# Identity products in TensorE's waits: one-head layers, and the scatter and gathering around layer 2's experts

## The reference

```python
# L1: gated attention over the context, one head of 128 features, 8 batches of 256 tokens
x = x + _L1_xattn_ref(_layernorm(x), ctx_1024, ctx_1024, Wgq, bgq, Wgk, bgk, w_gate, b_gate, Wh, bh)
...
# L2: causal attention over the context, one head
Q, K, V = q @ Wq, k @ Wk, v @ Wv
scores = where(causal, -inf, Q @ K.T / sqrt(128));  out = softmax(scores) @ V
# L2: 16 experts, two per token, at most 160 rows an expert
padded = zeros((16 * 160 + 1, 128)).at[slot].set(repeat(xf, 2, axis=0))   # the scatter
h = gelu(einsum('ecd,edf->ecf', padded, w1));  out_padded = einsum('ecf,efd->ecd', h, w2)
out = sum over the two choices of out_padded[slot] * weight               # the gathering
# L3: dilated attention: inside each segment softmax(x x^T / sqrt(128)) x, one head, divided by 4
x = x + _L3_attn_ref(_layernorm(x))
```

## Time and profile before

| | |
|---|---|
| time, median of 3 runs | 2066.54 us (2065.91 to 2067.85) |
| profiled execution | 2069.29 us, of which the trace's span is 2067.6 us |
| busy, share of the span | PE 80%, DVE 44%, ACT 34%, POOL 21% |
| granted TensorE clock, mean over the span | 0.901 of full speed |
| L1x begins | at 816.0 us of the span |
| L2x begins | at 1239.4 us |
| L2f begins (scatter), and its last product begins its group | at 1322.6 us; at 1453.6 us |
| L3a begins | at 1505.0 us |

### The profile page before, as it was taken

How to read it: one execution, slowest core, us unless ns; L and a number is a source line. 1 busy time by engine, 2 the same in 40 slices (tenths; PEclk the granted TensorE clock), 3 DMA queues, 4 the chain that set the end, 5 groups by cost and what they waited for, 6 DMA issues and landing times. The chain is left out here.

```text
span 2067.6 us, 31792 instructions
## 1 busy us (share of the span) xinstructions
PE 1643.8 (80%) x11656; PEld 963.7 (47%) x11656; DVE 911.0 (44%) x2515; ACT 711.5 (34%) x1423; POOL 436.8 (21%) x517
## 2 busy tenths in 40 slices
PE   1899899994799998869899987136156999969998
PEld 1344434443444444545644435124042555548887
DVE  3455345533355654641256535311354555324444
ACT  1244424442176775524213444011041333422221
POOL 2534043400121110000053400320515434100000
PEclk8999999997999998969999998567576999969999
DMA  8200000000000000000040000011200000000000
GB/s 235 67 2 1 1 1 1 1 1 0 0 1 1 1 1 1 1 0 1 4 148 2 1 1 1 20 53 52 59 12 6 12 12 6 1 0 0 0 0 20
DMA packets 45933, 37.63 MB, mean 18 GB/s; under 512 B 3972, under 2 KB 40040, under 8 KB 45800
## 3 DMA queue, kind: packets, MB, share of 16 engines
q1 hardware_dynamic: 43752, 31.65, 5.1%
q0 software_dynamic: 2048, 4.20, 0.7%
HBM read 23.26 MB, written 12.58 MB: 17 GB/s over the span
## 5 line engine op out<-in xcount | busy, mean ns | idle before, releaser
L1309 ACT ACTIVATE scores_L_experts_L<-L3x_psL 128x512 f32<-128x512 f32 x128 | 76.4, 597 | 173.8 <-PE L3x_psL L1172 170.2
L1346 DVE CUSTOM_DVE_ANT_0 L3x_junk<-L3x_psS,L3x_mask_rows 128x256 f32<-128x256 f32 x224 | 86.4, 422 | 92.6 <-PE L3x_psS L1134 84.5
L1172 PE MATMUL L3x_psL<-identb,L3x_mask_parts 128*128 128x256 bf16 x768 | 96.2, 276 | 0.0
L2433 ACT ACTIVATE L3f_activated<-L3f_psG 128x512 f32<-128x512 f32 x72 | 43.0, 597 | 153.0 <-PE L3f_psU L2412 153.0
L2466 DVE TENSOR_TENSOR L3f_hidden<-L3f_activated,L3f_psU 128x512 f32<-128x512 f32 x72 | 49.6, 688 | 103.0 <-ACT L3f_activated L2433 103.0
L852 ACT ACTIVATE L0x_probs<-L0x_psL 128x512 f32<-128x512 f32 x96 | 52.1, 595 | 114.1 <-PE L0x_psL L665 78.9
L852 ACT ACTIVATE L2a_probs<-L2a_psL 128x512 f32<-128x512 f32 x96 | 52.1, 595 | 104.2 <-PE L2a_psL L663 69.4
L852 ACT ACTIVATE L0a_probs<-L0a_psL 128x512 f32<-128x512 f32 x96 | 52.1, 595 | 100.8 <-PE L0a_psL L663 65.0
L1154 PE MATMUL L3x_psL<-L3x_qm,ctx_T 32*128 32x512 f32 x256 | 73.7, 651 | 12.1 <-DVE L3x_mx L1346 11.6
L2398 PE MATMUL L3f_psY<-experts_L_L,L3f_hidden 128*128 128x128 f32 x576 | 76.9, 276 | 5.0 <-DVE L3f_hidden L2466 4.9
L1172 PEld LDWEIGHTS L3x_psL<-identb,L3x_mask_parts 128*128 128x128 bf16 x768 | 70.4, 98 | 21.5 <-issue 13.7
(11 more groups left out here) (768 smaller groups left out, 4025.8 us busy)
## 6 DMA issues: line engine op xcount, KB each, us to landing
packed_rows<-zeros SPq DMA_DIRECT2D x1, 4608.0 KB, 27.2
L2f_rows<-packed_rows SPq DMA_DIRECT2D x8, 320.0 KB, 3.6
unpacked_rows<-L2f_y SPq DMA_DIRECT2D x8, 320.0 KB, 2.7
experts_L_L<-in_L_ffn_w_dram SPq DMA_DIRECT2D x1, 2048.0 KB, 8.5
unpacked_rows<-zeros SPq DMA_DIRECT2D x1, 2048.0 KB, 25.1
scores_L_experts_L<-in_L_ffn_w_dram SPq DMA_DIRECT2D x1, 2048.0 KB, 7.9
L3x_mask_rows<-in_mask_Bx1xSxS_ff_dram SPq DMA_DIRECT2D x8, 256.0 KB, 2.7
experts_L_L<-n_L_ffn_expert_gate_dram SPq DMA_DIRECT2D x1, 1024.0 KB, 13.4
```

Of the source, the lines that this page charges most:

```text
L1172: last = nc.tensor.matmul(at[:, :, t * P:(t + 1) * P], parts[:, b % 2, i, t, u * P:(u + 1) * P], two, start=False, stop=i == PARTS - 1, sk ...
L1309: nc.scalar.activation(probs[:, half, a, k, :], psL[i % RING][:], ACT.Exp).then_inc(s_prob, 1)
L1346: last = nc.vector.tensor_tensor_reduce(out=junk[:, i, :], in0=psS[a][:, i * S:(i + 1) * S], in1=mrow[:, b % 2, t, :], scale=1.0, scalar=L ...
```

## The change

A helper `warm(n)` is added to `lone_head` and to `slot_experts`, which issues n products of the identity into a bank that is overwritten before it is next read (`psS[1]` in the one, `psU[0]` in the other). `lone_head` issues 14 ahead of `turn(0)`, three after it, three after `turn(1)`, and three after `project(0)` where there is one. `slot_experts` issues 170 ahead of `turn(0)`, that is during the scatter, and 170 after the last `down`, that is during the gathering. Nothing is removed and no data changes.

```diff
@@ lone_head, TensorE
+                def warm(n):
+                    for _ in range(n):
+                        nc.tensor.matmul(psS[1][:], mem.identb[:], mem.identb[:].unsqueeze(1).to_broadcast([P, 4, P]), start=True, stop=True)
+
                 def turn(b):
                     pe.wait_ge(s_h, b + 1)
...
+                warm(14)
                 turn(0)
+                warm(3)
                 turn(1)
+                warm(3)
                 if not dilated:
                     project(0)
+                    warm(3)
                 for i in range(B + 2):
                     if i < B:
                         score(i)
@@ slot_experts, TensorE
+                def warm(n):
+                    for _ in range(n):
+                        nc.tensor.matmul(psU[0][:], mem.identb[:], mem.identb[:].unsqueeze(1).to_broadcast([P, 4, P]), start=True, stop=True)
+
...
                 pe.wait_ge(w["late"], w["late_count"])
+                warm(170)
                 turn(0)
                 for c in range(PAIRS + 1):
                     if c + 1 < PAIRS:
                         turn(c + 1)
...
                     if c >= 1:
                         down(c - 1)
+                pe.wait_ge(s_hid, UNITS * PAIRS)
+                warm(170)
```

## The result

The changed kernel takes **2098.91 us** (median, 2097.68 to 2101.22) against 2066.51 of the kernel before on the same chip: a ratio of 1.0157, 95% interval 1.014 to 1.0175, so 32.4 us longer. I had predicted 2069.7, 2065 to 2073: the loss is ten times the one forecast. The profiled execution took 2099.03 us, span 2097.3, which is 29.7 more than the span of before.

A forecast was written before the change was run, and what follows sets the result against it. At layer 2's experts TensorE waits for GpSimd's transfers; slow-clock starts of one-head layers were winnable. Those starts lose 8.8 us, regain 5.6, long runs 0: 2066.54 + 3.2 = 2069.7 us, range 2065 to 2073.

The forecast's parts named there:

- The 170 in the scatter: Layer 2's experts: products take 39.2 us, end at 1361.8 before rows arrive at 1368.17, nothing late: 0.
- the first pair starts slow as before: Experts' first pair: TensorE idles 6.4 us after the fillers, so its transposes start at the low clock again: 0.
- The cover: Layer 2's experts: the 45.6 us of the scatter, the wait in which the 170 products were to fit.
- The 170 in the gathering: End of layer 2's experts: 36.6 us at high clock, ending near 1491, 14 us before L3a: 0.
- Long fillers: Scatter and gathering: clock never rises for identities alone, making them 27 and 22 us late, about 2119; chance 0.04.
- the five waits in the loop over pairs: Experts' pair loop: TensorE idles 4.98 to 5.08 us for a load, five times, then transposes slowly.
- The 14 ahead of the first transposes: Starts of L1x, L2x, L3a: transposes 3.1, 2.8 and 2.8 or 2.9 us late, 8.8 us lost in all.
- What the one-head layers cost in all: Three one-head starts: 8.8 us lost, 5.6 us given back by the faster clock, 3.2 us net cost.
- From there on the clock is high in both kernels and the stages run as before, shifted: After the three one-head starts: later work keeps its length and is only shifted, adding no further term.
- The rival of moved code: Layer 2's attention: moved code costs by itself, 2.8 us longer (207.5 to 210.3); no chance given.

The follow-up runs named there:

- e_control: Changed kernel without its own products; 170 identity products in the stage just ahead of the scatter, no transfers beside them: 2092.02 us.
- e_heads: Changed kernel keeping only the 14 and 3s of the one-head layers, both runs of 170 left out: 2072.69 us, ratio 1.0024 to the kernel before.
- e_scatter: Changed kernel keeping only the 170 products in the scatter: 2079.11 us, ratio 1.0058 to the kernel before.
- e_gaps: Kernel before plus only 20 products in each of five 5 us waits of the experts' pair loop: 2055.86 us, ratio 0.9953.
- e_fit: Changed kernel with both runs of 170 cut to 80 and the one-head layers' products left out: 2068.57 us, ratio 1.0008 to the kernel before.

## Why the prediction was wrong, step by step

**The 170 in the scatter, the step that failed.** "So the first pair starts slow as before: 0. The cover is the 45.6 us of the scatter." The cover was about right: the rows lay ready 45.7 us behind the stage's start. The term that failed is the length set against it, "39.2 us and end at 1361.8", in which the transfers beside the products cost nothing. That is right where nothing holds TensorE, 39.30 us in e_control; beside the indirect transfers the 170 took 62.9 us. Some 90 pass, and what is left when TensorE is released again stands ahead of the rows' transposes: 67 products, 17.3 us late. That the first pair would start slow fell with it: it started late and at the high clock.

**The 170 in the gathering.** "Nothing waits for psU by then [...]: 0." The same step: the 170 took 63.8 us instead of 36.6, since 60 products were left at 1520.5, and the stage's end waited for them, 14.2 us.

**The rivals.** Long fillers that cost about 27 and 22 us were there, at 0.04, but for a clock that does not rise; it rose (the mean of 0.91 from 1326 to 1346 above). The place and the sign were those of this rival, the mechanism was another, which I had not thought of: I took a column of instructions without a wait for work that can't stop. One reading of the earlier trace rows was off as well, and moved no term of the sum: the five waits in the loop over pairs are 4.96 to 5.31 us long in the trace of before, not 4.98 to 5.08.

**The 14 ahead of the first transposes.** In L1x the mechanism and the size are right: transposes 6.19 us behind the table load, 2.82 before, so 3.4 late (3.1 predicted), and project(1) 1.9 later (1.8 predicted). In L2x they took 4.7 us, not 5.7, 1.9 us late instead of 2.8, and score(1) came 1.3 us earlier where I had 0. In L3a they went at full clock all along, since the long run had ended just ahead (a row above): 0.2 late, and the first weigh 1.2 earlier instead of 1.4 later. Timelines of TensorE and ScalarE:

```profile
815.89 5.63 PE L1904 MATMUL L1x_psS<-identb 128*128 128x512 bf16 x14
821.35 0.38 PE L1911 MATMUL L1x_psT<-ident,L1x_h 128*128 128x128 f32 x2
...
826.96 0.65 PE L1920 MATMUL L1x_psQ<-L1x_hT,wT_L_gq 128*64 128x256 f32 x2
...
1244.05 4.88 PE L1904 MATMUL L2x_psS<-identb 128*128 128x512 bf16 x14 [2.43 <-PEq L88]
1248.76 0.38 PE L1911 MATMUL L2x_psT<-ident,L2x_h 128*128 128x128 f32 x2
...
1256.14 0.46 PE L1944 MATMUL L2x_psS<-L2x_kT,L2x_qT 128*128 128x128 f32 x2 [0.61 <-ACT L2x_kT L2057]
...
1539.36 0.38 PE L1911 MATMUL L3a_psT<-ident,L3a_h 128*128 128x128 f32 x2
...
1545.81 1.16 PE L1982 MATMUL L3a_psO<-L3a_h,L3a_eT 128*128 128x128 f32 x8 [0.46 <-ACT L3a_eT L2074]
```

```profile
815.16 1.28 ACT L2032 ACT_TABLE_LOAD   x1 [7.82 <-PEq L88]
...
1244.01 1.28 ACT L2032 ACT_TABLE_LOAD   x1 [4.79 <-PEq L88]
...
1536.30 1.28 ACT L2032 ACT_TABLE_LOAD   x1 [70.49 <-PEq L88]
```

With steps of 0.425 and 0.215 us, 5.46 and 4.71 us are 12 and 8 products ahead of the rise. The prediction had quoted the Trainium skill (TensorE: Matmul & The Clock Gate, Part 1) on that number's changing from run to run, and set it aside; here it changes from layer to layer.

**What the one-head layers cost in all.** By e_heads 6.2 us, interval 2.5 to 7.6, where I had 3.2: inside, but not from the places that I had summed. "From there on the clock is high in both kernels and the stages run as before, shifted" is what doesn't hold. Stage lengths in us, from one table load to the next:

| stage | before | after | e_heads | e_scatter | e_gaps | e_fit |
|---|---|---|---|---|---|---|
| L1x | 57.00 | 58.91 | 58.90 | 56.98 | 59.15 | 59.18 |
| L2a | 207.51 | 210.30 | 210.34 | 207.51 | 210.55 | 210.57 |
| L2x | 45.76 | 44.42 | 44.41 | 45.73 | 43.66 | 43.65 |

Layer 2's attention, untouched, is 2.8 us longer in the changed kernel. The rival of moved code in e_heads' expectation would have had it so, but e_gaps and e_fit, which have no product ahead of that layer, show the same, and e_scatter, which has none either, does not. In it the clock falls where it held before (windows of 1 us, before and after, the same place in the program):

```profile
1069.00:1070.00 1.00, 1.00 (x10) 0.23 (x6) 0.47 (x2) 0.00 (x0) 0.00 (x0) 1.00 0.00 0
```

```profile
1071.00:1072.00 1.00, 1.00 (x8) 0.00 (x0) 0.30 (x1) 0.00 (x0) 0.00 (x0) 0.50 0.00 0
```

Two such falls, from 1070 to 1073.4 and from 1199.7 to 1203.1, are 6.8 us at half the clock. At most 3.4 us of work is lost in them, an estimate by these windows, which has room for the 2.8 us. And L1x is 2.2 us longer, L2x 2.1 shorter, without a single product there. So the few us of the one-head layers lie within what the clock's falls move from one build or run to another, and these runs don't settle what the 14 are worth in each.

**What stays open.** Shown is that 81 to 99 pairs of weight load and product, or 39 to 44 passes of the loop, go by before TensorE is held beside GpSimd's indirect transfers, that VectorE is held too, though sooner, and that no instruction fetch, no packet count and no plain transfer does it. In every run TensorE was released again only 1.5 to 4.0 us behind the issue of SyncE's load of the rows (in the scatter), and not when the last transfer had landed. What it is that fills, if anything does, is not shown, nor why indirect transfers bring it about. All timed runs of the changed kernels carry a span and a granted clock, so something was recorded in each, and the record that every instruction leaves is a candidate. The Trainium skill, in NOTIFIC — the notification-queue block, 7.1, says that the inner pipeline of the unit that writes such records makes its producers wait rather than lose one, and so could throttle an engine. No run here shows that it did, and none was without recording.

## What to carry to other kernels

A filler in a wait is free only if it is certain to be over when the wait ends: whatever of it is left stands in the engine's order ahead of the work that was waited for. So begin a filler on an event near the wait's end (the 26th of 32 transfers) and give it the size of what remains, instead of filling the whole wait from its start. And look first at the short waits that repeat, here five of 5 us: they gave 12.7 us in the stage, while 340 products in the two long waits cost 28.

## What the runs showed of the hardware that was not expected

- Beside GpSimd's indirect transfers TensorE came to a near stop after 81 to 99 products (0.08 to 0.45 us each), 72 to 90 of them behind the first transfer. From then on they went one or a few at a time, at multiples of 0.70 us. VectorE came to one after 55 stores, 15.3 us ahead of TensorE in the same run. Outside these transfers 170 products ran unbroken in 39.3 us.
- A one-product loop on TensorE takes 0.39 us a pass (four instructions) where the unrolled product takes 0.215, both at 2.4 GHz.
- One f32 product of 512 columns is booked as two pairs of weight load and product, 0.43 us each.
- Two builds that are alike up to layer 2's attention can differ by 2 to 3 us in a stage by where the granted clock falls.
